# Selective scan kernel: the gate moved from the output rows to the output weights, and from VectorE to GpSimd

## The reference, cut to what matters

```python
def step(h, inp):
    dt_t, B_t, C_t, u_t = inp
    dA = jnp.exp(dt_t[:, :, None] * A)
    h = h * dA + (dt_t * u_t)[:, :, None] * B_t[:, None, :]
    y = jnp.einsum('bdn,bn->bd', h, C_t)
    return (h, y)
...
y = jnp.transpose(ys, (1, 0, 2)) + u * D_param
y = y * jax.nn.silu(z)
return jnp.einsum('bsd,ed->bse', y, out_proj_w)
```

## Time and profile before

| | |
|---|---|
| median of 3 runs | 5542.39 us (5534.5 to 5546.62) |
| the profiled execution | 5539.89 us |
| its span | 5538.1 us |
| TensorE clock granted, mean | 0.97 |
| VectorE busy over the span | 4265.5 us |
| GpSimd busy over the span | 3596.6 us |
| share of the scan stage | the first 2130 us or so |

### The profile page before, as it was taken

The page is one execution under the profiler, slowest core; times in us unless marked ns, Lnnn a source line. Parts: engine busy times, 40 slices in busy tenths (PEclk is TensorE's granted clock), DMA queues, the critical chain, the costliest instruction groups (busy, mean ns, idle before and its releaser), DMA issues. The chain is left out here.

```text
span 5538.1 us, 62588 instructions
## 1 busy us (share of the span) xinstructions
PE 4962.2 (90%) x20224; PEld 2738.9 (49%) x20224; DVE 4265.5 (77%) x5656; ACT 3193.6 (58%) x5887; POOL 3596.6 (65%) x2406
## 2 busy tenths in 40 slices
PE   7888989898989877988999999999998888988998
PEld 2333333333333324764444444444443677776777
DVE  6999999999999995447777777777774565656565
ACT  3757575766667552225888888888886223232323
POOL 3879797978788773224889888988988322222222
PEclk9999999999999998997999999999999999999999
DMA  4021212211121203331111111111111412111212
GB/s 175 23 107 38 92 51 90 89 53 77 53 81 50 91 16 116 133 132 33 28 32 36 24 36 24 36 34 26 36 24 46 157 57 78 37 69 67 78 37 69
DMA packets 119638, 350.72 MB, mean 63 GB/s; under 512 B 13104, under 2 KB 14352, under 8 KB 104912
## 3 DMA queue, kind: packets, MB, share of 16 engines
q1 hardware_dynamic: 102448, 300.76, 16.8%
q0 software_dynamic: 9216, 33.56, 1.6%
q10 hardware_dynamic: 7648, 12.41, 0.7%
HBM read 278.49 MB, written 67.67 MB: 63 GB/s over the span
## 5 line engine op out<-in xcount | busy, mean ns | idle before, releaser
L431 POOL TENSOR_TENSOR mamba_hc<-mamba_h,mamba_bc 128x1024 f32<-128x1024 f32 x512 | 1217.0, 2377 | 353.6 <-DVE mamba_h L664 299.7
L812 PE MATMUL mamba_y<-mamba_hc,ident 128*128 128x512 f32 x2048 | 1004.7, 614 | 262.9 <-POOL mamba_hc L431 261.8
L1364 POOL TENSOR_TENSOR attn_pair_sum<-attn_pair_sum,attn_prob 128x1024 f32<-128x1024 f32 x512 | 1203.9, 2386 | 54.0 <-ACT attn_prob L1479 54.0
L1523 DVE TENSOR_REDUCE attn_mx<-attn_ps_max 128x1 f32<-128x512 f32 x1536 | 967.7, 685 | 317.2 <-PE attn_ps_max L1387 312.7
L1479 ACT ACTIVATE attn_prob<-attn_ps_s 128x512 f32<-128x512 f32 x2048 | 1051.3, 602 | 76.4 <-PE attn_ps_s L1414 76.4
L534 ACT ACTIVATE mamba_da<-mamba_dt,mamba_a_neg 128x512 f32<-128x512 f32 x1024 | 690.0, 689 | 692.7 <-DVE mamba_h L664 689.4
L664 DVE TENSOR_TENSOR_SCAN mamba_h<-mamba_da,mamba_state,mamba_h 128x512 f32<-128x512 f32 x768 | 940.1, 1266 | 1.9 <-ACT mamba_da L534 1.9
L1414 PE MATMUL attn_ps_s<-attn_q_stack,attn_k_stack 100*128 100x512 f32 x2048 | 884.9, 436 | 5.2 <-ACT attn_prob L1479 5.2
L1387 PE MATMUL attn_ps_max<-attn_k_stack,attn_q_stack 98*128 98x512 f32 x2048 | 833.2, 412 | 37.7 <-DMA attn_q_stack<-qk_parts 19.8
L812 PEld LDWEIGHTS mamba_y<-mamba_hc,ident 128*128 128x128 f32 x2048 | 371.4, 192 | 844.1 <-POOL mamba_hc L431 429.5
L654 DVE TENSOR_TENSOR mamba_h<-mamba_du,mamba_bc 128x1024 f32<-128x1024 f32 x512 | 619.6, 1210 | 65.5 <-POOL mamba_state L433 57.3
(11 more groups left out here) (302 smaller groups left out, 7475.1 us busy)
## 6 DMA issues: line engine op xcount, KB each, us to landing
mamba_bc<-bc_dram SPq DMA_DIRECT2D x64, 1024.0 KB, 7.3
mamba_w<-in_in_proj_w_T SPq DMA_DIRECT2D x16, 2048.0 KB, 7.8
qk_parts<-qkv_pair POOLq DMA_DIRECT2D x64, 512.0 KB, 3.2
attn_k_stack<-qk_parts SPq DMA_DIRECT2D x96, 256.0 KB
attn_q_stack<-qk_parts SPq DMA_DIRECT2D x96, 256.0 KB
mamba_x_in<-in_x SPq DMA_DIRECT2D x16, 1024.0 KB, 5.6
mamba_w<-in_out_proj_w_T SPq DMA_DIRECT2D x8, 2048.0 KB, 8.4
lin_norm_x<-x_after_L SPq DMA_DIRECT2D x16, 1024.0 KB, 5.6
```

The lines of the kernel that those rows point to most:

```text
L431: nc.gpsimd.tensor_tensor(hc[:, gs % HC_SLOTS, :, :], h[:, gs % H_SLOTS, :, :], bc[:, g, G:2 * G, :], ALU.mult).then_inc(s["hc_done"], 1)
L812: mm = nc.tensor.matmul(y[ct % 2][:, :], ident[:, :], hc[:, gs % HC_SLOTS, j, :], start=(g == 0 and j == 0), stop=(g == NG - 1 and j == G ...
L1364: nc.gpsimd.tensor_tensor(pair_sum[(hd * NGRP + g) % 2][:, at], first[:, at], prob[unit % SLOTS][:, at], ALU.add).then_inc(s["sum_done"], 1)
L1523: nc.vector.tensor_reduce(to, ps_max[seq % BANKS][:, :], AX.X, ALU.max, negate=own_block(i)).then_inc(s["bank_read"], 1)
```

## The change

The gate moves from the rows to the weights. Before, VectorE multiplied each finished bank of the output projection by the gate row and then added the residual rows: two operations for each of the four row tiles. Now the eight 128x512 slabs of w_out are multiplied in place by the gate row before the projection reads them, and VectorE adds the residual to the bank in one operation. The multiplications of the weights are GpSimd's, one at each of the steps 36, 41, 44, 49, 52, 55, 56 and 57. In the code they stand behind the step's `gate_y` and ahead of its `add_soft` and `add_tap`. TensorE waits for the slabs in place of the loaded weights.

```diff
+        GATE_W = {36: 0, 41: 1, 44: 2, 49: 3, 52: 4, 55: 5, 56: 6, 57: 7}
...
+            def gate_out(it, k):
+
+                if k == 0:
+                    q = turn_of["out", it]
+                    pool.wait_ge(w_in[q % 2], (q // 2 + 1) * 16)
+                    if it % NC_B == 0:
+                        wait_freed(pool, "cg", 0, it // NC_B)
+                w = w_view("out", it)[:, k, :]
+                nc.gpsimd.tensor_tensor(w, w, gate[:, it // NC_B, :], ALU.mult).then_inc(s["w_gated"], 1)
...
                     if i in GATE:
                         gate_y(it, GATE[i])
+                    if i in GATE_W:
+                        gate_out(it, GATE_W[i])
...
             def add_residual(it, t):

-                if it == 0 and t == 0:
-                    wait_freed(dve, "cg", 0, NB - 1)
                 bank = wait_full(dve, "out", it, t)
-                nc.vector.tensor_tensor(bank[:, :], bank[:, :], gate[:, it // NC_B, :], ALU.mult).then_inc(s["out_gated"], 1)
-                dve.wait_ge(s["out_gated"], it * TT + t + 1)
                 dve.wait_ge(s["residual_in"], (it + 1) * 16)
                 nc.vector.tensor_tensor(x_in[:, t, :], bank[:, :], x_in[:, t, :], ALU.add).then_inc(freed("out", it, t), 1)
...
             def project_back(it, t, part):
-                if t == 0 and part == 0:
-                    wait_weights("out", it)
+                if t == 0:
+                    pe.wait_ge(s["w_gated"], it * CT + 2 * part + 2)
                 pe.wait_ge(s["gated"], it * CT + 2 * part + 2)
```

More of the change, by code:

```diff
@@ L271, in stage_mamba @@
                  "drive_done exp_done scan_done state_saved hc_done sum_done y_read gated z_done tap_done tap_added u_done "
-                 "xp_read bc_written out_gated residual_in stored own_act own_norm setup_done zero_done "
+                 "xp_read bc_written w_gated residual_in stored own_act own_norm setup_done zero_done "
                  "u_begun gate_b_in cond_in small_in gate_w_in silu_done ident_done neg_done sum_set")
```

## The result

The changed kernel took 5573.29 us, the median of 7 runs (5566.28 to 5584.96), against 5543.95 us for the kernel before in 7 runs. The ratio is 1.0053, 95% interval 1.0041 to 1.0065: slower by 29 us. The forecast was 5571 us, +31.5 us on the profiled execution's own time; the profiled spans differ by 5571.4 - 5538.1 = 33.3 us.

The account below looks back on a forecast made before the run. GpSimd was taken to set the pace in steps 34 to 55, VectorE nearly everywhere else. +45.5 - 14.0 = +31.5 us on the profiled 5539.9 us gave 5571 us, range 5552 to 5586.

Parts of the forecast that it names:

- The window: Steps 34 to 55, at GpSimd's pace: the added multiplications cost 6.5 us in each of 7 chunks, 45.5 us.
- 41 and 49: Steps without a tap, where GpSimd makes good its lag: 1.23 us each less 0.16 us of idle time each.
- 55 to 57: Steps behind the window: GpSimd's step becomes 3.66 us against VectorE's 3.50, costing drives 58 and 59 some 0.26 us together.
- at step 47 it is as before: VectorE's dt times u product holds up the state copy longer at steps 39 and 55 only, 0.2 us twice a chunk.
- rival (d): Half hidden: ScalarE gains slack and tap pairs tighten by up to 1 us a chunk, 7 us less, 5564 us; 12%.
- The shut-out of VectorE's product: VectorE operations with two SBUF inputs and GpSimd operations reading SBUF exclude each other for a whole instruction; 0.4 us a chunk.
- The last chunk: No taps are added there, and bare steps follow the fullest ones: 0 us, bound 1 us.
- VectorE's saving: Gate multiplications gone at steps 7, 8, 12 and 16, those of 8 and 12 only partly saved: 12.8 us, bounds 5 and 19.9.
- rival (a): TensorE's clock does not fall behind its shorter wait at step 5, all 19.9 us are saved: 5564 us; 20%.
- The moved waits: Waits for w_out, the gate row and the slabs, and VectorE's dropped wait on its own multiplication: each costs nothing.
- The end: Behind the last chunk the last tile's gate goes and tile 0's bank comes free earlier: together 1.2 us saved.

Follow-up runs that it names:

- the kernel with this half alone: The kernel before plus the eight multiplications on GpSimd and TensorE's wait for them, VectorE still multiplying the rows: 5594.0 us, ratio 1.0077.
- the fastest kernel above: The changed kernel with multiplications at steps 32, 33, 55 to 58 and the next chunk's 0, 1, first residual addition at step 5, not 7: 5530.71 us, ratio 0.9973.
- VectorE's half alone: The changed kernel without the multiplications on GpSimd, the gate left out of the computation: 5534.54 us, ratio 0.9970.
- the kernel without the operations ahead of step 63: The changed kernel with multiplications at steps 32, 33, 55 to 58 and steps 0 and 1 of the next chunk: 5534.97 us, ratio 0.9985.

## Why the prediction was right, and where its terms were off

**The window, +45.5 us forecast.** Right in place, mechanism and size: 44.4 us in the seven chunks. That it is GpSimd's half is shown by the kernel with this half alone; that the steps decide is shown by the two with operations at 41 and 49 (+1.9 us) and at 55 to 57 (+0.2). Steps 41 and 49 were put at 2.1 us together, 55 to 57 at 0.26.

One reading in it was wrong: "at step 47 it is as before". VectorE's dt times u product of step 47 took 0.68 us before and 1.70 after, and there too the state copy was held up, to 0.65 us. So three copies a chunk were held up and not two, 21 x (252 - 184) ns = 1.4 us. A part of rival (d) came true against this: the tap additions lost the delays that VectorE's product gave them, 24 x (1313 - 1269) ns = 1.1 us. The prediction had this exchange at 0.4 us net, and it was 0.3.

**The shut-out of VectorE's product.** It was sized from steps 15 and 39, and this holds for the change itself, where the product took at most 1.77 us. As a bound for other places it is too low. The Trainium skill, "SBUF — State Buffer", section "SBUF: two separate sides", gives the pair of SBUF ports that VectorE and GpSimd share to whichever instruction starts first, for the whole instruction. The trace agrees with this where VectorE's product meets one product of GpSimd (2.54 us). It goes further where GpSimd's operations follow one another: there the wait lasted over up to three of them that read two tensors, 4.14 to 5.48 us.

**The last chunk, forecast 0, bound 1.** It cost 1.9 us, outside the bound. The forecast let GpSimd catch up in the bare steps behind each pair of extra operations. It hasn't by steps 39, 47 and 55: VectorE's product meets the last 0.6 us of GpSimd's 128x1024 product, waits for its end, and then holds up the state copy:

```profile
2100.38 2.35 POOL L442 TENSOR_TENSOR mamba_hc<-mamba_h,mamba_bc 128x1024 f32<-128x1024 f32 x1
...
2102.11 1.18 DVE L660 TENSOR_TENSOR mamba_du<-mamba_dt,mamba_u 128x512 f32<-128x512 f32 x1
2103.46 1.23 DVE L667 TENSOR_TENSOR mamba_h<-mamba_du,mamba_bc 128x1024 f32<-128x1024 f32 x1 [0.17 <-POOL mamba_state L444]
```

That is 1.18 for 0.67 us, and 0.17 us behind it, three times.

**VectorE's saving, 12.8 us forecast in the chunks.** It was 17.0 us: mis-sized, inside the bounds of 5 and 19.9. The mechanism was right. TensorE's late dt projection holds ScalarE, ScalarE holds GpSimd, and part of what VectorE saves at steps 7, 8 and 12 comes back at step 15. The step that failed is the size of this part, 1.42 us in each of three chunks and 0.9 in the last three.

The runs show the size. In the fastest kernel above, where nothing waits at step 15, tiles 0 to 3 take 123.1 us against 126.0: the four operations are worth 2.96 us a chunk, 20.7 us in all. So 3.7 us came back. The wait for the state copy at step 15 is 0.17 us in all seven chunks, where three had it (0.7 us more). The dt times u product ahead of it takes 0.77 to 1.23 us, where it took 0.68 to 0.89 (2.0 us more). In chunk 5 VectorE's scan waits for ScalarE's decay rows besides (1.0 us):

```profile
912.88 1.01 DVE L660 TENSOR_TENSOR mamba_du<-mamba_dt,mamba_u 128x512 f32<-128x512 f32 x1
914.06 1.23 DVE L667 TENSOR_TENSOR mamba_h<-mamba_du,mamba_bc 128x1024 f32<-128x1024 f32 x1 [0.17 <-POOL mamba_state L444]
...
1431.21 2.46 DVE L677 TENSOR_TENSOR_SCAN mamba_h<-mamba_da,mamba_state,mamba_h 128x512 f32<-128x512 f32 x2 [1.00 <-ACT mamba_da L547]
```

More than half of it stands in the duration of an instruction and not in a wait, as in the experiments.

It was less than forecast because TensorE's chain was shorter in most chunks. From the end of its wait to the dt projection were 892.22 - 871.98 = 20.2 us before and are 905.92 - 886.89 = 19.0 us after in the chunk that answers to it (TensorE in order of time):

```profile
886.89 3.65 PE L809 MATMUL mamba_work<-mamba_w,mamba_zy 128*128 128x512 f32 x4 [3.71 <-DVE mamba_x_in L691]
...
905.92 1.12 PE L799 MATMUL mamba_y<-mamba_dt_r,mamba_w_dt 64*128 64x512 f32 x2
```

The windows view behind the wait, of that chunk and of chunk 5, which saved least:

```profile
886.00:890.00 4.00, 3.11 (x4) 1.47 (x5) 4.00 (x5) 1.38 (x2) 2.48 (x2) 0.62 0.17 66
890.00:894.00 4.00, 4.00 (x10) 1.71 (x9) 4.00 (x5) 1.38 (x2) 2.49 (x2) 0.96 0.17 66
1406.00:1410.00 4.00, 3.51 (x4) 1.51 (x5) 4.00 (x5) 1.30 (x3) 2.46 (x3) 0.50 0.17 66
1410.00:1414.00 4.00, 4.00 (x8) 1.70 (x7) 4.00 (x5) 1.30 (x3) 2.40 (x3) 0.68 0.17 66
```

The clock fell behind every 3.7 us wait of this execution, so rival (a) did not come. It came back sooner in six chunks (0.62 and 0.96 in the one shown; 18.8 to 19.0 us to the dt projection) and later in one (0.50 and 0.68; 20.4 us). Before, six chunks had 20.0 to 20.4 us and one 18.7. The forecast took the long fall for the rule. Its three chunks of long fall were those of one execution of the kernel before. Over four profiled kernels each, with 28 such waits, the way to the dt projection is 18.7 to 20.4 us (mean 19.7) behind waits of 4.4 us and 17.3 to 20.4 us (mean 19.1) behind waits of 3.7 us. The shorter wait is followed by half a microsecond less on the average, but the ranges overlap, and what decides in a single chunk stays open. So the size of this saving hangs on the execution too: VectorE's half alone, with the same 3.7 us waits, saved 15.0 us in these tiles and not 17.0.

**The moved waits, 0 forecast.** Right: no instruction of TensorE waits for the slabs, and no operation of `gate_out` waited for its weights.

**The end, -1.2 us forecast, was -0.9.** The errors cancel in part: -1.1 in the window, +1.9 in the last chunk, -4.2 in the saving and +0.3 at the end make 28.4 us for the stage, 3.1 under the forecast. Another 4.8 us of the profiled difference come from parts that the change doesn't touch. That the profiled difference of 33.3 us lies so near to 31.5 is therefore luck in part. The median of the runs, +29.3 us, is near the stage's own figure.

## What to carry to other kernels

Read the pace stretch by stretch: an engine with 18% of idle time over a chunk was the bound for a third of it, and a step that looks free there is the one in which it makes good its lag. An operation that costs 1.23 us of GpSimd cost VectorE about its full length in that stretch and nearly nothing some steps later, so its place is worth more than its length.

When work goes to GpSimd, look at what VectorE runs beside it as well. An instruction of VectorE with two SBUF inputs should follow at once on what GpSimd too is waiting for, and not behind a run of GpSimd's operations; the delay shows in its duration, not in the waits.

## What the runs showed that was not expected

- VectorE's product of two SBUF tensors took 0.67 us when it came ahead of GpSimd's next operation, 1.18 and 1.70 us when it met the end of a 128x1024 product, 1.84 us when a tap addition started within 0.02 us of it (too close for the records to say which came first), 2.54 us when it came just after the start of a 128x1024 product, and 4.14 or 5.48 us when GpSimd's operations stood back to back. Why it was let in after the second operation in four chunks and only after all of them in three is open.
- TensorE's granted clock fell to 0.50 (1.2 GHz) behind all seven waits of 4.45 us before and all seven of 3.7 us after. In the kernel without the operations ahead of step 63 it fell behind five of the seven waits of 3.7 us and stayed at 1.00 behind the other two. It stayed at 1.00 where the wait was taken away. How long it stayed low differed between chunks of the same execution, and one chunk of the changed kernel was 1.4 us longer than its neighbours for it.
